# A hybrid conv, attention and LSTM kernel: output gate moved to partitions 64 to 127 of the cell gates' bank, table loads issued alone

## What is computed

```python
def step(carry, xs):
    h, c = carry
    xi_t, xf_t, xg_t, xo_t = xs
    i_t = jax.nn.sigmoid(xi_t + h @ V_i)
    g_t = jnp.tanh(xg_t + h @ V_c)
    o_t = jax.nn.sigmoid(xo_t + h @ V_o)
    c_new = h * c + i_t * g_t
    h_new = o_t * jnp.tanh(c_new)
    return ((h_new, c_new), h_new)
```

## Time and profile before

| what | value |
|---|---|
| median of 3 runs | 431.21 us (431.08 to 432.19) |
| the profiled execution: its own time | 431.55 us |
| its span, first to last instruction | 429.4 us |
| first gate sum of the recurrence | about 107 us into the span |
| TensorE, VectorE, ScalarE busy | 412.7, 245.8, 242.7 us |
| granted TensorE clock | 1.000 (the 2.4 GHz level) throughout |

### The profile page before, as it was taken

One profiled execution on the slowest core, in us unless ns is written; L12 is line 12 of the kernel. 1 busy time (PEld: TensorE's weight loads), 2 busy tenths in 40 slices (PEclk: granted clock), 3 DMA queues, 4 the chain that ended last, 5 costly groups with the idle time before them and its releaser, 6 DMA issues.

```text
span 429.4 us, 14807 instructions
## 1 busy us (share of the span) xinstructions
PE 412.7 (96%) x5669; PEld 232.9 (54%) x5669; DVE 245.8 (57%) x1160; ACT 242.7 (57%) x1142; POOL 59.5 (14%) x132
## 2 busy tenths in 40 slices
PE   8999997898999999999999999999999999999996
PEld 2555553555556565656556655656555656554443
DVE  2477745254665565656565656665566656564443
ACT  1666652663764676477647755775576467633332
POOL 6000004002110121112020202120111111120000
PEclk9999999999999999999999999999999999999999
DMA  7000000000000000000000000000000000000000
GB/s 240 0 2 2 2 2 0 0 3 0 5 2 2 5 5 5 2 5 3 3 2 5 5 2 4 5 4 2 2 5 3 2 5 4 4 2 5 2 2 5
DMA packets 2244, 3.78 MB, mean 9 GB/s; under 512 B 1277, under 2 KB 1726, under 8 KB 2174
## 3 DMA queue, kind: packets, MB, share of 16 engines
q1 hardware_dynamic: 1872, 2.32, 1.7%
q10 hardware_dynamic: 302, 0.52, 0.4%
HBM read 2.57 MB, written 0.26 MB: 7 GB/s over the span
## 4 chain that ended last, share of the span: by engine, by line
PE 74%; DVE 10%; ACT 10%; issue 4%; POOL 1%; DMA 1%; DVEq 0%; POOLq 0%
PE bank L352 20%; PE bank L625 18%; PE bank L481 7%; PE bank L419 5%; PE bank L407 5%; PE bank L492 4%; DVE bank L1044 4%; ACT SA L762 4%; PE bank L509 3%; DVE H L1054 3%; ACT bank L769 3%; PE bank L380 2%; PE bank L540 2%; ACT E L739 1%; PE bank L574 1%
## 5 line engine op out<-in xcount | busy, mean ns | idle before, releaser
L352 PE MATMUL bank<-FB 128*128 128x512 bf16 (+3 forms) x677 | 182.9, 367 | 1.2 <-DVE FB L795 1.2
L625 PEld LDWEIGHTS bank<-H,VW 128*32 128x32 f32 x3072 | 69.2, 111 | 82.6 <-DVE H L1054 78.6
L625 PE MATMUL bank<-H,VW 128*32 128x4 f32 x3072 | 91.8, 176 | 5.3 <-DVE H L1054 0.2
L1044 DVE TENSOR_TENSOR_SCAN bank<-SA 64x12 f32<-64x12 f32 x256 | 49.1, 192 | 72.8 <-ACT SA L762 71.3
L762 ACT ACTIVATE SA<-bank 64x8 f32<-64x8 f32 x256 | 44.7, 175 | 72.7 <-PE bank L625 71.9
L769 ACT ACTIVATE bank<-bank 64x4 f32<-64x4 f32 x256 | 38.4, 150 | 51.9 <-DVE bank L1044 51.9
L352 PEld LDWEIGHTS bank<-FB 128*128 128x128 bf16 x677 | 50.6, 99 | 30.1 <-issue 3.7
L1054 DVE SCALAR_TENSOR_TENSOR H<-TO,bank 64x4 f32<-64x4 f32 x256 | 40.8, 159 | 43.4 <-ACT bank L769 39.6
L336 POOL TENSOR_SCALAR E<-E,rinv 128x256 f32<-128x256 f32 x56 | 27.0, 482 | 145.4 <-DVE rinv L918 145.4
L1038 DVE SCALAR_TENSOR_TENSOR SA<-H,bank 64x4 f32<-64x4 f32 x256 | 41.3, 162 | 8.9
L481 PE MATMUL bank<-KF,QB 128*128 128x256 f32 x128 | 41.7, 407 | 1.7 <-DVE rinv L918 1.2
(11 more groups left out here) (117 smaller groups left out, 350.5 us busy)
## 6 DMA issues: line engine op xcount, KB each, us to landing
AW<-in_attn_w SPq DMA_DIRECT2D x1, 768.5 KB, 8.1
DW<-in_dcn_w SPq DMA_DIRECT2D x1, 576.0 KB, 6.6
X<-in_x_fm SPq DMA_DIRECT2D x1, 256.0 KB, 3.2
X<-in_x_fm ACTq DMA_DIRECT2D x1, 256.0 KB, 5.3
out_dram<-OUT SPq DMA_DIRECT2D x8, 32.0 KB, 1.4
CW<-in_conv_w SPq DMA_DIRECT2D x1, 243.5 KB, 3.8
VEC<-in_vecs SPq DMA_DIRECT2D x1, 160.0 KB, 8.0
K<-in_consts ACTq DMA_DIRECT2D x1, 154.0 KB, 3.4
```

The lines of the kernel that those rows point to most:

```text
L352: nc.tensor.matmul(idle[:, 0:n], FB[:, 0:P], FB[:, 0:n], start=True, stop=True)
L625: mm = nc.tensor.matmul(gate_out(m, gate, r, slice(B * s, B * (s + 1))), VW[:, gate, r], H[:, (STEPS * m + s - 1) % RING, :], start=False, ...
L1044: nc.vector.tensor_tensor_scan(CS.rearrange("p b q -> p (b q)"), SA[:, 0, :, :].rearrange("p b q -> p (b q)"), SA[:, 1, :, :].rearrange("p ...
```

## The change

Gate 2 gets the same two banks as gates 0 and 1, at partitions 64 to 127 beside gate 1's columns. Its matmuls, the preload and the recurrent part, are thus placed on the array's column groups 2 and 3 (output partitions 64 to 95 and 96 to 127), where they were on groups 0 and 1. Their order in the program stays: gate 0, gate 1, gate 2. The wait in `preload` goes. ScalarE's L766 now reads partitions 64 to 127. `table_for` and the scrap tile go; in its place stands `preload_act_table`, which issues an ACT_TABLE_LOAD and no activation.

```diff
-        scrap = sb("scrap", [1, 2 * NT])
 
         def gate_out(m, gate, rows, cols):
 
-            place = (0, P, P * (m % 2))[gate]
-            return (b_cell[m % 2] if gate < 2 else b_cs)[rows, place + cols.start:place + cols.stop]
+            half, place = ((0, 0), (0, P), (C, 0))[gate]
+            return b_cell[m % 2][half + rows.start:half + rows.stop, place + cols.start:place + cols.stop]
...
                 for gate in range(3):
-                    if gate == 2 and m >= 1:
-                        pe.wait_ge(o_gate, STEPS * m)
                     nc.tensor.matmul(gate_out(m, gate, slice(0, C), slice(0, P)), UW[:, gate, :],
...
-            def table_for(function, place):
-
-                nc.scalar.activation(scrap[:, place:place + 1], half_neg[0:1, 0:1], function)
-
...
                     if o == EXP_TABLE:
-                        table_for(ACT.Exp, 2 * m)
+                        nc.scalar.preload_act_table(ACT.Exp)
...
                     if o == GELU_TABLE:
-                        table_for(ACT.Gelu, 2 * m + 1)
+                        nc.scalar.preload_act_table(ACT.Gelu)
```

## The result

The changed kernel takes **428.47 us** (median, 428.44 to 429.23), the kernel before 431.19 on the same chip: 0.9936 of it, with a 95% interval of 0.9918 to 0.9954. That is faster by more than the 0.3% that a measurement here can tell. The prediction said 428.4, and 427.4 to 431.4. The profiled execution took 428.46 us, its span 426.6.

What follows compares the result with a forecast made beforehand. Most steps were taken as bound by the chain to H, some by TensorE. Gate 2's move gives -4.15 us, activations 0, the first load +1.30: -2.85 from 431.21 makes 428.4 us, range 427.4 to 431.4.

Steps and rivals of the forecast that it cites:

- Who ends last: Across 255 recurrence steps, only those where TensorE ends after H gain from shorter gate sums; the others gain nothing.
- The size of the gain, 0.063 a step: Twelve gate-sum passes end at 0.29 instead of 0.36 us; 49 turning steps give 3.09 us, seven gelu steps 0.44.
- exp pairs: In six exp steps QB waits for the fills' end and the next tanh for QB; earlier fills gain 0.38 us.
- the last preload: In tile 7 gate 2's preload passes, 0.22 us, run beside the rest; gain 0.24 us, then H is late next.
- weighing's four at a time: Weighing's passes on four column groups run four together, 0.03 us apart; gate 2's were expected to run likewise beside gate 0's.
- The wait for `o_gate`: In the preload, this wait costs nothing by itself; the passes behind it take the time.
- Gate 1 isn't delayed: Gate sums: no delay assumed; the rival, a delay of 0.032 us per step, gave 434.4 us, chance 0.06.
- The activation is worth nothing: Dropping the 1x1 activation behind 13 recurrence table loads gains 0, since ScalarE's 0.22 us each goes into waiting.
- The first load, +1.30: The new load before tile 0's queries, its set already in place, takes 1.28 us and costs 1.30 us.
- The rival of a free load: The load of the set in place before tile 0's queries costs nothing: 427.1 us, chance 0.06.
- L759 "at the same 0.16": Sign of being right: gate 2's tanh on ScalarE reads 64 partitions of a cell bank at the same 0.16 us.
- The clock: TensorE idles 0.06 more in 1.17 us, but the granted clock is 1.000 in all stages; no chance of its own.

Runs made afterwards that it cites:

- experiment 4: Changed kernel with gate 2 in the third bank (partitions 64 to 127), its wait restored, cell state and its tanh at partitions 0 to 63: 421.55 us.
- experiment 5: Changed kernel with only the cell state and its tanh moved to partitions 0 to 63 of the third bank: 421.66 us.
- Experiment 8: Changed kernel with gate 2's matmuls issued ahead of those of gates 0 and 1: 434.25 us.
- experiment 2: Kernel before with table loads issued alone, without the activation, gates untouched: 431.74 us against 430.72.
- experiments 9 and 10: Fewer fills in table-load steps (NS_TABLE 700, not 900): changed kernel 425.49 us; kernel before with only gate 2 moved 426.22 us in one profiled execution.

## Why the prediction was right

- **Who ends last.** The sorting of the steps into those that end with H and those that end with TensorE carried the whole sum. All terms that it gave a gain gained. Of the others, the seven feed-forward steps and the steps that end with H stayed, but for small delays.
- **The size of the gain, 0.063 a step.** Measured 0.062 in 49 turning steps (3.03 of 3.09), 0.064 in the gelu steps (0.45 of 0.44), 0.37 of 0.38 in the exp pairs, 0.24 of 0.24 at the last preload. The step from weighing's four at a time to the gates holds: a later matmul on free column groups doesn't wait for an earlier pass whose group is taken. The Trainium skill ("TensorE: Matmul & The Clock Gate", What overlaps and what doesn't) has matmuls start and end strictly in program order. For the starts the trace disagrees: four passes more fit into the same 0.29 us, and the one that raises `o_mm` starts ahead of gate 1's last. For the ends the signals agree: `o_mm` rises at 0.378, behind `ig_mm` at 0.319.
- **The wait for `o_gate`** costs nothing, as said: experiment 4 has it and its last preload step is as short as that of experiment 5.
- **Gate 1 isn't delayed**: the tanh comes at 0.34. Experiment 8 shows that this hangs on gate 2 standing last.
- **The activation is worth nothing** in the recurrence: experiment 2. The cover named, the fills, is the right one: experiments 9 and 10. Outside the span the activations cost some 0.3 us, which the sum lacked.
- **The first load, +1.30**: measured +1.33 in the trace. The rival of a free load is out.
- **L759 "at the same 0.16"** was wrong: 0.172, and 0.20 behind the first tanh, not 0.07. ScalarE then idles less ahead of L762 (15.8 us in all), but L762 waits for the scan, so it was hidden.
- **The sum.** -4.15 + 1.30 = -2.85 was forecast, and the medians differ by 2.72. That it comes so close is in part luck. The two profiled executions differ by 3.09: the steps that were to gain gave 4.09, the load cost 1.33, the steps that were to stay lost 0.72, 0.24 were gained outside the span, and 0.76 are the earlier rise of the clock in the second execution, together 3.04. The last three aren't in the forecast, and they partly cancel.
- **The clock** was taken as 1.000 in all stages. It was at its lower level up to 9.74 us; the forecast doesn't rest on that stretch, but it moved the convolution's first matmul by 0.76 us between the two executions.

What the prediction didn't see at all is the larger gain beside it: that the chain it took as given, 1.17 us from sums to sums, holds 0.025 that come from the cell state's partitions.

## What to carry to other kernels

Sort the steps of a loop by what ends last in each, and give a gain only to those in which the shortened engine does; when a planned filler is what ends a step, nothing behind it is worth anything until the filler is cut, and a plan fitted to the old instruction times should be fitted again. Put matmuls that nobody waits for on column groups that are free, behind those that somebody waits for. Try small PSUM and SBUF tiles on a path of dependent operations at partitions 0 to 63 first: it was worth 7 us here for the cell state and 15 for SA, and nothing for TO. Don't load a table that is in place.

## What the runs showed of the hardware that was not expected

- Operations on 64x4 and 64x12 elements took 7 to 10 ns longer with an operand in PSUM at partitions 64 to 127 (scan 192 and 183 ns, H 160 and 150, L762 152 and 143), the second tanh some 15 (172 and 156). The cause is open.
- Two operations in a row on ScalarE or VectorE overlap by 0.05 to 0.10 us or follow with a gap of 0.02 to 0.03, depending on the partitions of the small one and on what its neighbour touches. Between the best and the worst placement of SA and the cell state lie 21.6 us (421.7 and 443.3).
- Passes of later matmuls start between earlier ones on other column groups, 2 to 25 ns apart, while those of gates 0 and 1 keep their distances (0.05, then 0.03). The semaphores still rise in program order.
- A load of the set in place takes 1.28 us, as one that changes it.
- The clock rose 9.74 us into the span in one profiled execution and at 4.31 in the other, and eight fills at 6 us took 3.57 and 1.89 us accordingly. The views show 1.00 in both there, since no entry stands ahead of the rise. What decides its moment is open.
